# Graph layer on one core: the first group's user products in rounded and remainder parts, with buffers that share the left-over rows' place

## Chip, cores and metric

The kernel runs on 1 core of one Trainium2 chip. The metric is the device time of one execution in microseconds (us); before the change the median of 3 runs is 1091.55 us (1091.31 to 1091.62). The engines are TensorE (PE in the rows; PEld are its weight loads), VectorE (DVE), ScalarE (ACT), GpSimd (POOL) and SyncE (SP), which here only issues loads and stores.

## What is computed

```python
def ref(x, item_feat, adj, W_item, b_item, W_user, b_user):    # 10000 users, 10000 items, width 128
    u = maximum(layernorm(x, eps=1e-5), 0.0)
    h = item_feat @ W_item.T + b_item
    b = u @ W_user.T + b_user
    return x + relu(adj @ h + b)
```

Everything is float32. The adjacency is 10000 x 10000, 400 MB, read once.

## The kernel before

**Tiling.** The output is computed transposed, 128 features on the partitions and users along the free axis. Users are cut in five groups of 2048 (the last has 1808), each held in four PSUM banks of 512 (the very last bank has 272). Items are cut in 78 tiles of 128; 16 are left over. So the kernel walks 5 x 78 = 390 adjacency tiles of 128 items x 2048 users, 1 MB each. "Tile 60" below means tile 60 of its group.

**One tile.** SP loads it to one of eight slots of `a_ring` (L273), when tile n-8 has been used. ScalarE rounds it to `hi_ring` (float32r, four slots, L382), VectorE subtracts that from the tile and writes the remainder over the tile, as `lo_ring` (L496), and TensorE makes three matmuls for each of the four banks: h_lo x hi (L795), h_hi x hi (L796), h_hi x lo (L802). In the first 12 tiles of group 0 the pieces are halves or quarters (L390, L505).

**h.** In group 0 h is made beside the tiles, a trio of 128-item blocks at a time: three float32 matmuls (L721) at each third tile up to tile 69, which show as six instructions; then VectorE adds the bias (L523), ScalarE rounds (L403), VectorE takes the remainder (L534). The item features come in pieces of 384 KB (L265), one at each sixth tile in SP's order.

**The layer norm of x.** POOL issues loads of the users' rows to `rows` (L323; in group 0 four pieces of 256 KB when ScalarE has rounded 14, 16, 18 and 20 tiles: `ROWS_AT`), and of x to `y` (L326). VectorE sums rows (L572), TensorE makes the means (L740), VectorE centres (L580), ScalarE squares (L449), VectorE sums the squares (L587), TensorE makes variances (L746), VectorE adds eps, ScalarE takes the root, VectorE corrects and inverts it (L598 to L606), then scales and clamps (L612) and transposes (L619) one bank's users at a time to `normed_t`.

**The user product.** In group 0 it is one float32 matmul per bank (L754, `user_product`). In groups 1 to 4 it is made of parts (L762, L763, L765, `user_parts`): ScalarE rounds `normed_t` to `turned_hi` (L434), VectorE takes the remainder `turned_lo` (L566), and three float32r matmuls follow. These buffers lie over `items`, the item features' buffer, which is free only after group 0; W_user is rounded and subtracted early in group 1 (L417, L552).

**Left-over items.** Their 16 rows of the adjacency, three times, and two rows of ones for the bias come as four loads of 100 KB a group (L281, `load_rem`), ScalarE rounds them in two parts (L426), VectorE subtracts in two (L557), TensorE makes four matmuls of 50 rows (L776).

**Order.** Each engine runs its program in order. The place of each step is a tile number in the tables `FIRST` (group 0) and `LATER` (groups 1 to 4) and in constants such as `WU_AT`; a step stands before its tile's matmuls on TensorE and behind its tile's rounding or subtraction on ScalarE and VectorE. Steps for the four banks follow each other at `NORM_EVERY` = 5 tiles, the row sums at 2, the two parts of the left-over rows at 4.

## Time and profile before

| | us |
|---|---|
| median of 3 runs | 1091.55 (1091.31 to 1091.62) |
| the profiled execution | 1091.64 |
| its span, first to last instruction | 1089.8 |
| TensorE busy | 1084.4 |
| VectorE busy | 989.2 |
| ScalarE busy | 776.2 |
| POOL busy | 33.7 |
| chain that ended last | TensorE 99% |

Matmuls are pipelined and a matmul's end in the record is modelled: one shows as some 0.39 us while the next starts after about 0.23. So durations of TensorE are read here as distances between starts. A row of the timeline has the start and the time in us, the engine, line, operation, what it writes and reads, and, where the engine was idle before it, for how long and what ended that. The granted TensorE clock is full in all stretches.

### The profile page before, as it was taken

What the parts mean: (1) busy time and instruction counts of PE and PEld (TensorE: products, weight loads), DVE (VectorE), ACT (ScalarE), POOL (GpSimd) and SP (SyncE); (2) the same over time, 40 slices, a digit from 0 to 9 for tenths busy, and PEclk for the clock granted to TensorE, in tenths of its full rate; (3) what the DMA queues carried; (4) which work ended last, traced back from release to release, by engine and by line L of the source; (5) the groups of instructions that cost most, each with busy time, mean ns of one, the idle gap of its engine ahead of it and who ended that gap; (6) DMA issues with size and microseconds to landing.
All of it is one profiled execution on the core that took longest, in us unless ns stands there. A gap on an engine that the chain in (4) does not pass through costs nothing.

```text
span 1089.8 us, 12092 instructions
## 1 busy us (share of the span) xinstructions
PE 1084.4 (100%) x4952; PEld 900.4 (83%) x4952; DVE 989.2 (91%) x640; ACT 776.2 (71%) x492; POOL 33.7 (3%) x67
## 2 busy tenths in 40 slices
PE   9999999999999999999999999999999999999998
PEld 7888888788888888888888888888888888888887
DVE  7989999999899998898999988989999889899986
ACT  6767777667777776677777766777777667777764
POOL 0000000000000000000000000000000000000000
PEclk9999999999999999999999999999999999999999
DMA  9999999999999999999999999999999999999994
GB/s 387 416 425 407 424 426 375 372 358 410 410 399 407 379 400 388 376 415 400 400 395 390 399 380 357 424 413 394 403 387 399 363 364 413 385 414 393 384 346 149
DMA packets 65193, 422.98 MB, mean 388 GB/s; under 512 B 7977, under 2 KB 8778, under 8 KB 25202
## 3 DMA queue, kind: packets, MB, share of 16 engines
q1 hardware_dynamic: 60386, 407.61, 93.3%
q0 software_dynamic: 4608, 14.46, 4.3%
q8 instruction: 39, 0.64, 0.2%
q14 instruction: 16, 0.13, 0.0%
q10 hardware_dynamic: 144, 0.13, 0.0%
HBM read 417.04 MB, written 5.12 MB: 387 GB/s over the span
## 4 chain that ended last, share of the span: by engine, by line
PE 99%; DVE 0%; DMA 0%; ACT 0%; DVEq 0%; issue 0%
PE acc L795 32%; PE acc L802 32%; PE acc L796 32%; PE acc L721 2%; PE acc L762 0%; PE acc L765 0%; PE acc L763 0%; PE acc L754 0%; DMA wi_bi<-in_w_item_and_bias 0%; PE acc L776 0%; PE acc L706 0%; DVE y L630 0%; DVE lo_ring L505 0%; ACT hi_ring L390 0%; PE acc L740 0%; PE acc L746 0%
## 5 line engine op out<-in xcount | busy, mean ns | idle before, releaser
L382 ACT CAST hi_ring<-a_ring 128x2048 fp32r<-128x2048 f32 (+1 forms) x378 | 708.3, 1874 | 289.8 <-PE acc L802 266.2
L496 DVE TENSOR_TENSOR lo_ring<-a_ring,hi_ring 128x2048 fp32r<-128x2048 f32 (+1 forms) x378 | 840.7, 2234 | 78.8 <-ACT hi_ring L382 76.5
L795 PE MATMUL acc<-hi_ring,h_lo 128*128 128x512 f32 (+1 forms) x1560 | 604.5, 387 | 0.0
L802 PE MATMUL acc<-lo_ring,h_hi 128*128 128x512 f32 (+1 forms) x1560 | 599.9, 385 | 0.2 <-DVE lo_ring L505 0.2
L796 PE MATMUL acc<-hi_ring,h_hi 128*128 128x512 f32 (+1 forms) x1560 | 600.0, 385 | 0.0
L795 PEld LDWEIGHTS acc<-hi_ring,h_lo 128*128 128x128 f32 x1560 | 293.2, 188 | 59.7 <-issue 2.7
L802 PEld LDWEIGHTS acc<-lo_ring,h_hi 128*128 128x128 f32 x1560 | 292.9, 188 | 59.5 <-DVE lo_ring L505 0.8
L796 PEld LDWEIGHTS acc<-hi_ring,h_hi 128*128 128x128 f32 x1560 | 293.1, 188 | 57.8 <-issue 0.7
L505 DVE TENSOR_TENSOR lo_ring<-a_ring,hi_ring 128x1024 fp32r<-128x1024 f32 (+1 forms) x28 | 28.7, 1068 | 2.3 <-ACT hi_ring L390 2.3
L390 ACT CAST hi_ring<-a_ring 128x1024 fp32r<-128x1024 f32 (+1 forms) x28 | 24.5, 925 | 6.6 <-DMA a_ring<-in_adj_tiles 6.6
L326 POOL DMA_DIRECT2D y<-in_x_t x20 | 10.8, 542 | 530.0 <-ACT hi_ring L382 530.0
L721 PEld LDWEIGHTS acc<-wi_bi,items 128*128 128x128 f32 x156 | 21.9, 196 | 2.9 <-DMA wi_bi<-in_w_item_and_bias 0.9
L721 PE MATMUL acc<-wi_bi,items 128*128 128x128 f32 x156 | 22.4, 281 | 0.6 <-DMA wi_bi<-in_w_item_and_bias 0.6
L323 POOL DMA_DIRECT2D rows<-in_x_slices x20 | 10.9, 543 | 276.2 <-DVE normed_t L619 215.7
L523 DVE TENSOR_TENSOR h_full<-acc,wi_bi 128x384 f32<-128x384 f32 x25 | 13.8, 552 | 4.6 <-PE acc L721 4.4
L630 DVE SCALAR_TENSOR_TENSOR y<-acc,y 128x512 f32<-128x512 f32 (+1 forms) x20 | 12.7, 672 | 4.2 <-PE acc L802 4.2
L619 DVE STREAM_TRANSPOSE normed_t<-rows 128x512 f32<-128x512 f32 (+1 forms) x20 | 14.0, 700 | 0.7
L534 DVE TENSOR_TENSOR h_lo<-h_full,h_hi 128x384 fp32r<-128x384 f32 x25 | 13.8, 550 | 0.0
L403 ACT CAST h_hi<-h_full 128x384 fp32r<-128x384 f32 x25 | 12.7, 507 | 1.5 <-DVE h_full L523 1.5
L612 DVE SCALAR_TENSOR_TENSOR rows<-rows,stat 128x512 f32<-128x512 f32 (+1 forms) x20 | 13.5, 673 | 0.0
L580 DVE TENSOR_TENSOR rows<-rows,acc 128x512 f32<-128x512 f32 (+1 forms) x20 | 13.3, 667 | 0.0
L587 DVE TENSOR_REDUCE stat<-normed_t 128x16 f32<-128x512 f32 (+1 forms) x20 | 13.3, 666 | 0.0
(55 smaller groups left out, 153.9 us busy)
## 6 DMA issues: line engine op xcount, KB each, us to landing
a_ring<-in_adj_tiles SPq DMA_DIRECT2D x312, 1024.0 KB, 7.6
a_ring<-in_adj_tiles SPq DMA_DIRECT2D x78, 904.0 KB, 6.8
rows<-in_x_slices POOLq DMA_DIRECT2D x19, 256.0 KB, 6.9
y<-in_x_t POOLq DMA_DIRECT2D x19, 256.0 KB, 6.9
items<-in_item_t SPq DMA_DIRECT2D x12, 384.0 KB, 11.1
out_t<-y POOLq DMA_DIRECT2D x16, 256.0 KB, 7.8
a_rem<-in_adj_rem SPq DMA_DIRECT2D x20, 100.0 KB
out_t<-y SPq DMA_DIRECT2D x3, 256.0 KB, 2.4
```

The source lines that it names most:

```text
L382: nc.scalar.copy(hi_ring[:, n % S_SLOTS, cols], a_ring[:, n % A_SLOTS, cols]).then_inc(hi_written, 1)
L390: nc.scalar.copy(hi_ring[:, r, cols], a_ring[:, s, cols]).then_inc(part_hi if part < parts - 1 else hi_written, 1)
L496: nc.vector.tensor_tensor(lo_ring[:, s, cols], a_ring[:, s, cols], hi_ring[:, r, cols], ALU.subtract).then_inc(lo_written, 1)
L505: nc.vector.tensor_tensor(lo_ring[:, s, cols], a_ring[:, s, cols], hi_ring[:, r, cols], ALU.subtract).then_inc(part_lo if part < parts - 1 ...
L523: nc.vector.tensor_tensor(h_full[:, trio % H_BANKS, :, :], h_banks[trio % H_BANKS][:, 0:TRIO_W].rearrange("p (c d) -> p c d", d=HID), bi.u ...
L534: nc.vector.tensor_tensor(h_lo[:, trio * TRIO:(trio + 1) * TRIO, :], h_full[:, trio % H_BANKS, :, :], h_hi[:, trio * TRIO:(trio + 1) * TRI ...
L612: nc.vector.scalar_tensor_tensor(out=rows[:, b, :], in0=rows[:, b, :], scalar=0.0, in1=inv[:, b].unsqueeze(2).broadcast_to(wide(b)), op0=A ...
L619: nc.vector.transpose(normed_t[:, 0:n, :], rows[:, b, :]).then_inc(normed_t_ready, 1)
L721: last = nc.tensor.matmul(out, items[:, slot, at:at + P], wi, start=(m == 0 or (trio, m) == (0, 1)), stop=True, skip_group_check=True)
L795: nc.tensor.matmul(acc[k][:, 0:bank_w(g, k)], h_lo[:, c, :], hi, start=(c == 0), stop=False, skip_group_check=True)
L796: nc.tensor.matmul(acc[k][:, 0:bank_w(g, k)], h_hi[:, c, :], hi, start=False, stop=False, skip_group_check=True)
L802: last = nc.tensor.matmul(acc[k][:, 0:bank_w(g, k)], h_hi[:, c, :], lo, start=False, stop=(c == CHUNKS - 1), skip_group_check=True)
```

## The change

- The user products of group 0 are made by `user_parts` too; `user_product` is gone. ScalarE rounds `normed_t` at tiles 59, 64, 69, 74 of group 0, VectorE subtracts at 60, 65, 70, 75, and the products stand at 62, 67, 72, 77 (before: 61, 66, 71, 76).
- `turned_hi` and `turned_lo` lie over `a_rem` and `rem_parts`, the buffers of the left-over rows, and no more over `items`. So the left-over product stands ahead of the user products (tile 52 of group 0 and 46 of the others, before 66), ScalarE's first two roundings of a group wait for it, and the load of a group's left-over rows waits for the user products of the group before; it is issued at tile 24 instead of 30.
- W_user is rounded at tile 38 of group 0 instead of tile 4 of group 1.
- In group 0 all of the norm's steps stand two or three tiles earlier, and the rows' loads two. In the later groups norm, roundings and products stand two tiles later, and the left-over rows' rounding and subtraction 5 to 6 tiles earlier.

```diff
-REM_AFTER = 30
+REM_AFTER = 24
-WU_AT = 4
+WU_AT = 38
-ROWS_AT = 14
+ROWS_AT = 12
-FIRST = {"sum": 22, "mean": 30, "centre": 32, "square": 35, "sum_squares": 36, "wide_every": 4, "var": 51, "eps": 54, "sqrt": 57,
-         "root": 58, "norm": 59, "user": 61, "rem_round": 50, "rem_subtract": 52, "rem": 66}
+FIRST = {"sum": 20, "mean": 28, "centre": 30, "square": 33, "sum_squares": 34, "wide_every": 4, "var": 48, "eps": 51, "sqrt": 54,
+         "root": 55, "norm": 56, "turned": 59, "turned_lo": 60, "user": 62, "rem_round": 40, "rem_subtract": 43, "rem": 52}
 LATER = {"sum": 6, "mean": 15, "centre": 18, "square": 21, "sum_squares": 22, "wide_every": 5, "var": 40, "eps": 43, "sqrt": 46,
-         "root": 47, "norm": 50, "turned": 53, "turned_lo": 54, "user": 57, "rem_round": 38, "rem_subtract": 40, "rem": 66}
+         "root": 47, "norm": 52, "turned": 55, "turned_lo": 56, "user": 59, "rem_round": 32, "rem_subtract": 35, "rem": 46}
...
+        rem_at = nc.sbuf_base
         a_rem = sb("a_rem", [P, PAIR, BANK_W])
         rem_parts = sb("rem_parts", [P, PAIR, BANK_W], F32R)
+        turned_hi = nc.alloc_sbuf_tensor_at("turned_hi", [P, 2, BANK_W], F32R, offset=rem_at)
+        turned_lo = nc.alloc_sbuf_tensor_at("turned_lo", [P, BANK_W], F32R, offset=rem_at + 2 * BANK_W * 4)
...
-        items_at = nc.sbuf_base
         items = sb("items", [P, ITEM_SLOTS, PIECE_W])
-        turned_hi = nc.alloc_sbuf_tensor_at("turned_hi", [P, 2, BANK_W], F32R, offset=items_at)
-        turned_lo = nc.alloc_sbuf_tensor_at("turned_lo", [P, BANK_W], F32R, offset=items_at + 2 * BANK_W * 4)
...
             def load_rem(g):
                 if g > 0:
-                    sp.wait_ge(rem_lo_set, PAIR * g)
+                    sp.wait_ge(user_done, UNITS * g)
...
             def turned_round(g, k):
...
-                if v >= 2:
+                if k < 2:
+                    act.wait_ge(rem_used, g + 1)
+                else:
                     act.wait_ge(user_done, u - 1)
...
                     k = unit_at(c, at_of(g, "user"), NORM_EVERY)
-                    if k is not None and g == 0:
-                        user_product(g, k)
-                    elif k is not None:
+                    if k is not None:
                         user_parts(g, k)
```

Three places of the engines' order show what moved. On TensorE, around the first user product of group 0 (tile 61 before, tile 62 after), before:

```order
L802 MATMUL acc<-lo_ring,h_hi 128x512
L754 MATMUL acc<-normed_t,wu 128x512
L795 MATMUL acc<-hi_ring,h_lo 128x512
L796 MATMUL acc<-hi_ring,h_hi 128x512
L802 MATMUL acc<-lo_ring,h_hi 128x512
```

and after, where L783, L784 and L790 are the three matmuls of a bank:

```order
L790 MATMUL acc<-lo_ring,h_hi 128x512
L750 MATMUL acc<-turned_hi,wu_lo 128x512
L751 MATMUL acc<-turned_hi,wu_hi 128x512
L753 MATMUL acc<-turned_lo,wu_hi 128x512
L783 MATMUL acc<-hi_ring,h_lo 128x512
```

One float32 matmul has become three float32r matmuls. On SP, at tiles 18 to 36 of group 0 (L265 is a piece of the item features, L281 the left-over rows), the difference:

```order
 L265 DMA items<-in_item_t 128x768
 L273 DMA a_ring<-in_adj_tiles 128x2048 x6
-L265 DMA items<-in_item_t 128x768
-L273 DMA a_ring<-in_adj_tiles 128x2048 x6
 L281 DMA a_rem<-in_adj_rem 50x512 x4
 L265 DMA items<-in_item_t 128x768
```

The four loads stand six adjacency tiles and one piece of the item features earlier. On VectorE, from tile 58 to tile 61 of group 0 in the changed kernel (L496 are tiles, L534 and L523 belong to h, L611 and L615 are one bank's norm and transposition):

```order
L496 TENSOR_TENSOR lo_ring<-a_ring,hi_ring 128x2048
L523 TENSOR_TENSOR h_full<-acc,wi_bi 128x384
L496 TENSOR_TENSOR lo_ring<-a_ring,hi_ring 128x2048 x2
L534 TENSOR_TENSOR h_lo<-h_full,h_hi 128x384
L565 TENSOR_TENSOR turned_lo<-normed_t,turned_hi 128x512
L496 TENSOR_TENSOR lo_ring<-a_ring,hi_ring 128x2048
L523 TENSOR_TENSOR h_full<-acc,wi_bi 128x384
L611 SCALAR_TENSOR_TENSOR rows<-rows,stat 128x512
L615 STREAM_TRANSPOSE normed_t<-rows 128x512
```

and before, from tile 61 to tile 64, around the second bank's norm:

```order
L523 TENSOR_TENSOR h_full<-acc,wi_bi 128x384
L496 TENSOR_TENSOR lo_ring<-a_ring,hi_ring 128x2048 x2
L534 TENSOR_TENSOR h_lo<-h_full,h_hi 128x384
L496 TENSOR_TENSOR lo_ring<-a_ring,hi_ring 128x2048
L523 TENSOR_TENSOR h_full<-acc,wi_bi 128x384
L612 SCALAR_TENSOR_TENSOR rows<-rows,stat 128x512
L619 STREAM_TRANSPOSE normed_t<-rows 128x512
```

A subtraction of 512 columns has come in one tile ahead of each norm but the first, and one behind the last.

## Rows read from the trace of the kernel before

**Rows 1.** Head of the page: span, and busy time of TensorE and its weight loads.

```profile
span 1089.8 us, 12092 instructions
...
PE 1084.4 (100%) x4952; PEld 900.4 (83%) x4952; DVE 989.2 (91%) x640; ACT 776.2 (71%) x492; POOL 33.7 (3%) x67
```

**Rows 2.** Timeline, VectorE's subtraction and TensorE's first use, tiles 20, 24 to 26.

```profile
65.69 2.29 DVE L496 TENSOR_TENSOR lo_ring<-a_ring,hi_ring 128x2048 fp32r<-128x2048 f32 x1
...
69.05 0.39 PE L802 MATMUL acc<-lo_ring,h_hi 128*128 128x512 f32 x1
...
77.88 2.29 DVE L496 TENSOR_TENSOR lo_ring<-a_ring,hi_ring 128x2048 fp32r<-128x2048 f32 x1 [0.91 <-ACT hi_ring L382]
...
81.15 2.28 DVE L496 TENSOR_TENSOR lo_ring<-a_ring,hi_ring 128x2048 fp32r<-128x2048 f32 x1
...
81.33 0.40 PE L802 MATMUL acc<-lo_ring,h_hi 128*128 128x512 f32 x1
...
84.02 2.27 DVE L496 TENSOR_TENSOR lo_ring<-a_ring,hi_ring 128x2048 fp32r<-128x2048 f32 x1
...
84.09 0.39 PE L802 MATMUL acc<-lo_ring,h_hi 128*128 128x512 f32 x1
...
86.81 0.39 PE L802 MATMUL acc<-lo_ring,h_hi 128*128 128x512 f32 x1
```

**Rows 3.** Waits: who, for whom, us in total, times, longest us.

```profile
ACT hi_ring L382 <- DMA a_ring<-in_adj_tiles: 23.1, 25, 2.6
```

**Rows 4.** Timeline of TensorE, either side of a user product, tile 61, group 0.

```profile
190.96 0.40 PE L802 MATMUL acc<-lo_ring,h_hi 128*128 128x512 f32 x1
...
192.29 0.39 PE L796 MATMUL acc<-hi_ring,h_hi 128*128 128x512 f32 x1
```

**Rows 5.** Timeline of TensorE, group 1: around left-over product and user parts.

```profile
425.20 0.39 PE L802 MATMUL acc<-lo_ring,h_hi 128*128 128x512 f32 x1
...
426.52 0.39 PE L796 MATMUL acc<-hi_ring,h_hi 128*128 128x512 f32 x1
...
428.81 0.40 PE L802 MATMUL acc<-lo_ring,h_hi 128*128 128x512 f32 x1
...
429.75 0.39 PE L795 MATMUL acc<-hi_ring,h_lo 128*128 128x512 f32 x1
```

**Rows 6.** Timeline of TensorE, group 0: around a trio, around tile 66's pieces.

```profile
197.29 0.39 PE L802 MATMUL acc<-lo_ring,h_hi 128*128 128x512 f32 x1
...
198.41 0.40 PE L796 MATMUL acc<-hi_ring,h_hi 128*128 128x512 f32 x1
...
206.17 0.39 PE L802 MATMUL acc<-lo_ring,h_hi 128*128 128x512 f32 x1
...
209.01 0.39 PE L796 MATMUL acc<-hi_ring,h_hi 128*128 128x512 f32 x1
```

**Rows 7.** Timeline of ScalarE: roundings of tiles 20, 21 and 24, group 0.

```profile
63.74 1.92 ACT L382 CAST hi_ring<-a_ring 128x2048 fp32r<-128x2048 f32 x1 [0.84 <-DMA a_ring<-in_adj_tiles]
66.19 1.92 ACT L382 CAST hi_ring<-a_ring 128x2048 fp32r<-128x2048 f32 x1 [0.53 <-DMA a_ring<-in_adj_tiles]
...
75.93 1.92 ACT L382 CAST hi_ring<-a_ring 128x2048 fp32r<-128x2048 f32 x1 [1.62 <-DMA a_ring<-in_adj_tiles]
```

**Rows 8.** Groups by form: count, then busy us, mean ns, idle us before.

```profile
L566 DVE TENSOR_TENSOR turned_lo<-normed_t,turned_hi 128x512 fp32r<-128x512 f32 x15 | 10.3, 686 | 0.3
```

**Rows 9.** Timeline around tile 60: first norm, tile, piece of h; TensorE's use.

```profile
184.18 0.68 DVE L612 SCALAR_TENSOR_TENSOR rows<-rows,stat 128x512 f32<-128x512 f32 x1
...
185.53 2.25 DVE L496 TENSOR_TENSOR lo_ring<-a_ring,hi_ring 128x2048 fp32r<-128x2048 f32 x1
...
187.70 0.55 DVE L534 TENSOR_TENSOR h_lo<-h_full,h_hi 128x384 fp32r<-128x384 f32 x1
...
188.16 2.29 DVE L496 TENSOR_TENSOR lo_ring<-a_ring,hi_ring 128x2048 fp32r<-128x2048 f32 x1
...
188.88 0.40 PE L802 MATMUL acc<-lo_ring,h_hi 128*128 128x512 f32 x1
```

More of the change, by code:

```diff
@@ L428, in turned_round @@
             def turned_round(g, k):
-                u, v, n = g * UNITS + k, (g - 1) * UNITS + k, bank_w(g, k)
+                u, n = g * UNITS + k, bank_w(g, k)
                 act.wait_ge(normed_t_ready, u + 1)
-                if v >= 2:
+                if k < 2:
+                    act.wait_ge(rem_used, g + 1)
+                else:
                     act.wait_ge(user_done, u - 1)
-                nc.scalar.copy(turned_hi[:, v % 2, 0:n], columns_of(normed_t)[:, 0:n]).then_inc(turned_hi_set, 1)
+                nc.scalar.copy(turned_hi[:, k % 2, 0:n], columns_of(normed_t)[:, 0:n]).then_inc(turned_hi_set, 1)
             def square(g, k):
@@ L442, in square @@
                     act.wait_ge(squares_summed, u)
-                elif g == 1:
-                    act.wait_ge(user_done, u)
-                elif g > 1:
-                    act.wait_ge(turned_lo_set, u - UNITS)
+                elif g > 0:
+                    act.wait_ge(turned_lo_set, u)
                 nc.scalar.activation(squares[:, 0:n, :], rows[:, b, :], ACT.Square).then_inc(squares_ready, 1)
@@ L474, in _ @@
                         h_rem_round()
-                    if g == 1 and c == WU_AT:
+                    if g == 0 and c == WU_AT:
                         wu_round()
@@ L483, in _ @@
                         root_of_var(g)
-                    k = unit_at(c, at_of(g, "turned"), NORM_EVERY) if g > 0 else None
+                    k = unit_at(c, at_of(g, "turned"), NORM_EVERY)
                     if k is not None:
@@ L550, in wu_subtract_lo @@
                 dve.wait_ge(wu_hi_set, 1)
-                dve.wait_ge(user_done, UNITS)
                 nc.vector.tensor_tensor(wu_lo[:, :], wu[:, :], wu_hi[:, :], ALU.subtract).then_inc(wu_lo_set, 1)
@@ L560, in turned_subtract @@
             def turned_subtract(g, k):
-                u, v, n = g * UNITS + k, (g - 1) * UNITS + k, bank_w(g, k)
-                dve.wait_ge(turned_hi_set, v + 1)
-                if v > 0:
+                u, n = g * UNITS + k, bank_w(g, k)
+                dve.wait_ge(turned_hi_set, u + 1)
+                if k > 0:
                     dve.wait_ge(user_done, u)
-                nc.vector.tensor_tensor(turned_lo[:, 0:n], columns_of(normed_t)[:, 0:n], turned_hi[:, v % 2, 0:n],
+                nc.vector.tensor_tensor(turned_lo[:, 0:n], columns_of(normed_t)[:, 0:n], turned_hi[:, k % 2, 0:n],
                                         ALU.subtract).then_inc(turned_lo_set, 1)
@@ L615, in norm @@
                 dve.wait_ge(normed_ready, u + 1)
-                if g == 0 and k > 0:
-                    dve.wait_ge(user_done, u)
                 nc.vector.transpose(normed_t[:, 0:n, :], rows[:, b, :]).then_inc(normed_t_ready, 1)
@@ L673, in _ @@
                         empty(g - 1, 3)
-                    if g == 1 and c == WU_AT + 1:
+                    if g == 0 and c == WU_AT + 1:
                         wu_subtract_lo()
@@ L693, in _ @@
                         norm(g, k)
-                    k = unit_at(c, at_of(g, "turned_lo"), NORM_EVERY) if g > 0 else None
+                    k = unit_at(c, at_of(g, "turned_lo"), NORM_EVERY)
                     if k is not None:
@@ L747, in variance_product @@
                                  skip_group_check=True).then_inc(variance_done, 1)
-            def user_product(g, k):
-                if (g, k) == (0, 0):
-                    pe.wait_ge(user_loaded, 2 * 16)
-                pe.wait_ge(normed_t_ready, g * UNITS + k + 1)
-                columns = columns_of(normed_t)[:, 0:bank_w(g, k)]
-                nc.tensor.matmul(acc_of(g)[k][:, 0:bank_w(g, k)], wu[:, :], columns, start=False, stop=False,
-                                 skip_group_check=True).then_inc(user_done, 1)
             def user_parts(g, k):
-                u, v, n, out = g * UNITS + k, (g - 1) * UNITS + k, bank_w(g, k), acc_of(g)[k]
-                if v == 0:
+                u, n, out = g * UNITS + k, bank_w(g, k), acc_of(g)[k]
+                if u == 0:
                     pe.wait_ge(wu_lo_set, 1)
-                pe.wait_ge(turned_hi_set, v + 1)
-                nc.tensor.matmul(out[:, 0:n], wu_lo[:, :], turned_hi[:, v % 2, 0:n], start=False, stop=False, skip_group_check=True)
-                nc.tensor.matmul(out[:, 0:n], wu_hi[:, :], turned_hi[:, v % 2, 0:n], start=False, stop=False, skip_group_check=True)
-                pe.wait_ge(turned_lo_set, v + 1)
+                pe.wait_ge(turned_hi_set, u + 1)
+                nc.tensor.matmul(out[:, 0:n], wu_lo[:, :], turned_hi[:, k % 2, 0:n], start=False, stop=False, skip_group_check=True)
+                nc.tensor.matmul(out[:, 0:n], wu_hi[:, :], turned_hi[:, k % 2, 0:n], start=False, stop=False, skip_group_check=True)
+                pe.wait_ge(turned_lo_set, u + 1)
                 nc.tensor.matmul(out[:, 0:n], wu_hi[:, :], turned_lo[:, 0:n], start=False, stop=False,
```

## The prediction, as put on record before the changed kernel ran

> **What bounds the kernel now.** I read the head of the profile's page first: TensorE is busy for 1084.4 of the 1089.8 us of the span [rows 1]. The reader is to see that nothing but work taken off TensorE, or a stall put into it, can move the end. A busy PE need not be a PE at its pace, so I then read the timeline of PE for the distance between the starts of neighbouring matmuls. In the plain stretch that I use it is about 0.227 us (tile 20's L802 at 69.05, tile 25's at 84.09 and tile 26's at 86.81: between the last two lie 12 matmuls in 2.72 us) [rows 2]. The list of waits is read next, for ScalarE, which rounds each tile and stands between the loads and the rest: it waits for loads of the adjacency 25 times, 23.1 us in all [rows 3]. Nearly all of these waits belong to the first group, while the ring of eight tiles is being filled, and there the kernel is thin.
>
> So two things have to be worked out: what TensorE does less, and whether the moved loads and VectorE work run into the short lead that VectorE has over TensorE in the first group.
>
> **The TensorE sum.** A user product of group 0 is one float32 matmul in the code. Its cost is read between its neighbours: the L802 before it starts at 190.96, the L796 behind it at 192.29, 1.33 us apart, where two steps of 0.227 would be 0.45. The product costs 0.88 us [rows 4]. A product in parts, in group 1, runs from L802 at 428.81 to L795 at 429.75, 0.94, less one step: 0.71 us [rows 5]. The left-over product alone costs 1.32 - 0.45 = 0.87 (425.20 to 426.52) [rows 5]. The three matmuls of a trio cost 1.12 - 0.45 = 0.67 (197.29 to 198.41). At tile 66 a trio, a user product and the left-over product stand together and cost 2.84 - 0.45 = 2.39 (206.17 to 209.01), which is 0.03 less than 0.67 + 0.88 + 0.87 [rows 6]; the change separates them.
>
> Before: 3 x 0.88 + 2.39 = 5.03. After: 4 x 0.71 + 0.87 + 0.67 = 4.38. TensorE has 0.65 us less to do. Matmuls behind such a piece keep for one tile a pace about 0.003 us slower, so I hold 0.5 to 0.7 for possible. In the groups 1 to 4 the same matmuls are issued at other tiles: their left-over product goes from tile 66, next to nothing, to tile 46, next to nothing, the user parts from 57 to 59, and both cost what they did. Their sum is 0.
>
> The Trainium skill, page "TensorE: Matmul & The Clock Gate", section Back-to-back issue gap, gives N/2.4 + 2.5 ns for a warm matmul, 216 ns for 512 columns. By it three parts would cost 0.65 and the four products 0.9 us less instead of 0.7. The trace disagrees in every plain stretch, 0.227 for a step [rows 2], and the row decides.
>
> **What lies beside TensorE: ScalarE.** It gets four roundings of 512 columns more in group 0, of the kind of L434, and these lie where it waits for PE: it needs 1.92 us for a tile of 2.72 [rows 7]. Its new wait for the left-over product (tile 52, needed at 59) is met long before, as ScalarE is two to three tiles ahead of PE. Cost 0; behind it on ScalarE stand only the roundings of the ring, whose lead is several us there.
>
> **VectorE at the end of group 0.** It gets four subtractions, 0.69 us each for 15 of their kind in the later groups [rows 8]. The thin place before is tile 60, after the root and the first norm: its subtraction ends at 185.53 + 2.25 = 187.78, and PE wants it at 188.88, a lead of 1.10 [rows 9]. The root and norm move by three tiles, a whole trio period, so the same dip comes at tile 57. From there a round of five tiles costs VectorE, read from start to start, 5 x 2.17 (185.53 to 187.70), 5/3 x 2 x 0.46 for the pieces of h (187.70 to 188.16), 1.35 for a norm (184.18 to 185.53) [rows 9] and at most 0.69 for the new subtraction: 14.4 us. TensorE takes 5 x 2.72 + 5/3 x 0.67 + 0.71 = 15.4. The lead grows by 1.0 a round, so I take 0. If the cover is gone, the bound is 4 x 0.69 = 2.8 us; the lower end is 0, as nothing is taken from VectorE there. The left-over subtractions at 43 and 47 replace those at 52 and 56, where the lead is as large.
>
> **The loads and sums at tiles 12 to 27.** Here the change costs something. Tiles land 2.45 us apart while ScalarE waits for them (63.74 and 66.19, both ended by the load) [rows 7]: the DMA engines are full. A 256 KB piece of rows or x, a quarter of a tile, thus pushes later tiles back by 0.61 us, and the 400 KB of left-over rows push by 0.96. Four pieces of rows are issued two tiles earlier, and the x piece behind them with them. At tile 20 all five will have gone, before three had: the tile lands up to 2 x 0.61 = 1.2 us later. VectorE's lead there is 69.05 - (65.69 + 2.29) = 1.07 [rows 2]. The stall is then 0.15.
>
> The left-over rows go ahead of tile 24 instead of tile 30. VectorE's lead at tile 24 is 81.33 - (77.88 + 2.29) = 1.16; 0.96 of it goes and the earlier stall gives 0.15 back: 0.35. From tile 24 to 25 VectorE needs 81.15 - 77.88 = 3.27 (a subtraction of h and a row sum stand between them, in both kernels) and PE 84.09 - 81.33 = 2.76: 0.51 is lost, and the stall is about 0.15. To tile 26 VectorE needs 84.02 - 81.15 = 2.87 against 2.72, another 0.15. Before, the lead at tile 26 was 86.81 - (84.02 + 2.27) = 0.52, and nothing stalled [rows 2]. Together 0.45 us. The bound below is 0, if the transfers find gaps. The bound above is all of it on the path: 1.2 + 0.96 + one row sum moved ahead, at most 0.6 by the 3.27 + the 0.3 of the last two steps = 3.1. I take 0.45, by the leads, since they are read at the very tiles.
>
> That the pieces share the engines is also the rule of the Trainium skill, page "DMA: Bandwidth & Descriptors", section Issuing engines are not separate DMA queues: transfers of all issuing engines run on the same 16 and interleave. It speaks against this change, for by it the earlier rows on the POOL queue cannot pass beside the ring. The trace agrees as far as it can: ahead of tile 24, with a piece of items and two pieces from the POOL queue under way, ScalarE waits 1.62 us for the load, where it waits 0.53 for tile 21 [rows 7].
>
> **Queues and edges.** SP's new wait stands ahead of tile 24 of a group and asks for the user products of the group before, done about 18 tiles earlier; behind it wait the ring's loads, and they lose nothing. W_user's two halves move from group 1 to tile 38 and 39 of group 0, some 0.3 us each on engines with a lead. The first ten tiles and the tail after the last matmul are not touched.
>
> **The sum.** -0.65 + 0.45 = -0.2 us. The execution in the profile took 1091.64 (span 1089.8, so 1.84 outside), and this would give 1091.4; the median of 1091.55 gives 1091.35. I predict 1091.4. What a measurement of this kernel can tell from no change is about 0.2%, 2.2 us, so this is no change.
>
> **The rivals.**
> - *The leads hold* (chance 0.33). The saving of TensorE comes out whole: 1091.55 - 0.65 = 1090.9. For it: the lead of 1.07 and 1.16 nearly covers each delay, and pieces issued by POOL may be served slowly, not all at once. Against it: the lead of 0.52 at tile 26 is smaller than the 0.96 of the left-over rows.
> - *VectorE becomes the bound at the end of group 0* (0.09). If a round of five tiles has no 1.0 us to spare, up to 2.8 us of the new subtractions come on the path, less the lead of 1.1: 1091.55 - 0.65 + 1.7 = 1092.6, still within 0.2%.
> - *The ring runs dry* (0.04), the case on the slower side. At tiles 18 to 27 the leads cover nothing and the whole delay comes on the path: 1091.55 - 0.65 + 3.1 = 1094.0. It decides where the stalls of these tiles pass 2.8 us; with the lead of 1.16 spent first, tile 24 would have to land 4 us later than at 75.93. For it: the wait of 1.62 us shows what a few small loads do to one tile [rows 7]. Against it: the moved bytes add up to 2.2 us, and these leads are real in the rows.
> - *TensorE changes its pace* (0.02). With no float32 product in a group's last 17 tiles the products' neighbours would go faster than I read; for 0.2% that would have to be 2.2 us in 17 tiles, and no row shows such a pace.
>
> **How the numbers follow.** The forecast (stall and saving nearly cancel) has 0.52. Its own range is 1090.9 to 1092.1. With the first rival and the bound of the second the range is 1090.7 to 1092.6, and it leaves out about 0.1. Slower by over 0.2% is the third rival, 0.04; faster by over 0.2% is the last, 0.02; the rest, 0.94, is no change.
>
> **What would show it.** In the changed profile a user product of group 0 is three matmuls about 0.23 us apart, and the distance from the matmul before to the one behind is one step plus 0.71. Tile 20 and tiles 24 to 26 start late: the L802 of one of them begins as VectorE's subtraction ends, and ScalarE waits for its load at 24 longer than 1.62 us. From tile 57 to 77 PE has no wait. Groups 1 to 4 take the same time as before to 0.1 us. The forecast is wrong if the first group is longer than before by over 1 us, or shorter by over 1 us, or if any later group differs.

## The result, and the profile after

| | before | changed |
|---|---|---|
| median | 1091.62 us (12 runs, 1091.31 to 1092.46) | 1094.39 us (12 runs, 1093.36 to 1094.81) |
| ratio to before | | 1.0023, 95% interval 1.0016 to 1.0031 |
| profiled execution | 1091.64, span 1089.8 | 1094.03, span 1092.2 |

The changed kernel is slower by 0.23%, 2.8 us between the medians, and the interval leaves out 1. The forecast was 1091.4, the range 1090.7 to 1092.6, and "slower" had a chance of 0.04.

The head of the page after answers to [rows 1]. TensorE has four matmuls more, since the four user products of group 0 are now in parts, and is busy 1.5 us longer:

```profile
span 1092.2 us, 12109 instructions
...
PE 1085.9 (99%) x4956; PEld 901.1 (83%) x4956; DVE 990.1 (91%) x644; ACT 778.5 (71%) x496; POOL 33.7 (3%) x67
```

On so full an engine the busy time doesn't say where the loss is, because the end of a matmul that waits is also counted. The list of waits of the changed kernel (engine, line, for whom: us in total, times, longest) does. TensorE stands in it with new entries for VectorE's subtraction, and ScalarE's wait for tiles has become rarer than in [rows 3], 19 times and not 25, without the sum falling as much:

```profile
ACT hi_ring L382 <- DMA a_ring<-in_adj_tiles: 20.7, 19, 2.7
...
PEld acc L790 <- DVE lo_ring L496: 2.5, 4, 1.1
...
PE acc L790 <- DVE lo_ring L496: 0.9, 2, 0.6
```

To place it, I took the distance between the first matmuls of neighbouring tiles in both profiles. A stall is what such a distance has more than before:

| stretch | after minus before, us | forecast |
|---|---|---|
| up to tile 12 of group 0 | +0.43 | not touched |
| stalls at tiles 20, 24, 25, 26 | +0.38 +0.88 +0.57 +0.11 = +1.94 | +0.45 |
| the rest of group 0 | -0.53 | -0.65 |
| groups 1, 2, 3 | 0.00 each (216.49 and 216.49) | 0 |
| group 4 | +0.56 (190.27 to 190.83) | 0 |
| sum | +2.40 | -0.2 |

The first line can't be put down to the change: over the profiles of all kernels here the start of tile 12 lies anywhere from 44.8 to 45.7 us, in kernels with the rows of x at 14 (44.9 to 45.6) as in those with them at 12 (44.8 to 45.7).

**Group 0.** The timeline of ScalarE after (start, duration, what it waited for), tiles 20 to 24, answers to [rows 7]:

```profile
65.40 1.91 ACT L382 CAST hi_ring<-a_ring 128x2048 fp32r<-128x2048 f32 x1 [1.51 <-DMA a_ring<-in_adj_tiles]
67.82 1.91 ACT L382 CAST hi_ring<-a_ring 128x2048 fp32r<-128x2048 f32 x1 [0.51 <-DMA a_ring<-in_adj_tiles]
70.26 1.92 ACT L382 CAST hi_ring<-a_ring 128x2048 fp32r<-128x2048 f32 x1
74.01 1.92 ACT L382 CAST hi_ring<-a_ring 128x2048 fp32r<-128x2048 f32 x1 [1.83 <-DMA a_ring<-in_adj_tiles]
78.63 1.91 ACT L382 CAST hi_ring<-a_ring 128x2048 fp32r<-128x2048 f32 x1 [2.70 <-DMA a_ring<-in_adj_tiles]
```

The left-over rows are issued ahead of tile 24. Here tile 23 lands 3.75 us behind tile 22, and tile 24 another 4.62 us later, where a plain tile takes 2.44. VectorE and TensorE then, tiles 24 to 26, against [rows 2]:

```profile
80.57 2.29 DVE L496 TENSOR_TENSOR lo_ring<-a_ring,hi_ring 128x2048 fp32r<-128x2048 f32 x1 [2.21 <-ACT hi_ring L382]
83.85 2.28 DVE L496 TENSOR_TENSOR lo_ring<-a_ring,hi_ring 128x2048 fp32r<-128x2048 f32 x1
86.71 2.27 DVE L496 TENSOR_TENSOR lo_ring<-a_ring,hi_ring 128x2048 fp32r<-128x2048 f32 x1
```

```profile
82.92 0.50 PE L790 MATMUL acc<-lo_ring,h_hi 128*128 128x512 f32 x1 [0.63 <-DVE lo_ring L496]
86.18 0.50 PE L790 MATMUL acc<-lo_ring,h_hi 128*128 128x512 f32 x1 [0.26 <-DVE lo_ring L496]
...
89.06 0.48 PE L790 MATMUL acc<-lo_ring,h_hi 128*128 128x512 f32 x1
```

Each first use begins 0.05 to 0.08 us behind the end of the subtraction (80.57 + 2.29 = 82.86, and 82.92): the lead of 1.16 us is gone. VectorE's own steps are those of before, 3.28 and 2.86 us (3.27 and 2.87 in [rows 2]). Only the landing of tile 24 moved.

**Group 4.** Its banks are 272 columns wide at the end. The first of the three matmuls on such a bank, once per tile, before:

```profile
1014.52 0.28 PE L795 MATMUL acc<-hi_ring,h_lo 128*128 128x272 f32 x1
...
1016.95 0.28 PE L795 MATMUL acc<-hi_ring,h_lo 128*128 128x272 f32 x1
```

and after, first behind the left-over product at tile 46, then behind the user products at tiles 59 and 64:

```profile
1012.46 0.29 PE L783 MATMUL acc<-hi_ring,h_lo 128*128 128x272 f32 x1
...
1014.93 0.29 PE L783 MATMUL acc<-hi_ring,h_lo 128*128 128x272 f32 x1
...
1055.54 0.28 PE L783 MATMUL acc<-hi_ring,h_lo 128*128 128x272 f32 x1
...
1057.96 0.28 PE L783 MATMUL acc<-hi_ring,h_lo 128*128 128x272 f32 x1
```

A tile takes 2.47 us at first and 2.42 later, with no wait in the rows. The step is 2.467 us from tile 47 up to tile 58 and 2.420 before the left-over product: 11 x 0.047 = 0.52 of the 0.56.

### The profile page after: what moved, and what is told of

Read it like the earlier page. It is cut to its first block, busy times and chain, and to the rows that moved or that the text cites. A ratio compares the mean times of both kernels' runs of the same rounds, so it can differ in the third digit from the quotient of the medians.

```text
span 1092.2 us, 12109 instructions
## 1 busy us (share of the span) xinstructions
PE 1085.9 (99%) x4956; PEld 901.1 (83%) x4956; DVE 990.1 (91%) x644; ACT 778.5 (71%) x496; POOL 33.7 (3%) x67
## 4 chain that ended last, share of the span: by engine, by line
PE 96%; DMA 2%; DVE 1%; ACT 0%; DVEq 0%; issue 0%
PE acc L783 31%; PE acc L790 31%; PE acc L784 31%; DMA a_ring<-in_adj_tiles 2%; PE acc L717 1%; PE acc L750 0%; PE acc L753 0%; PE acc L751 0%; DVE lo_ring L496 0%; DMA wi_bi<-in_w_item_and_bias 0%; PE acc L764 0%; ACT hi_ring L382 0%; PE acc L702 0%; DVE y L626 0%; DVE lo_ring L505 0%; PE acc L736 0%
## 5 line engine op out<-in xcount | busy, mean ns | idle before, releaser
L496 DVE TENSOR_TENSOR lo_ring<-a_ring,hi_ring 128x2048 fp32r<-128x2048 f32 (+1 forms) x378 | 840.6, 2233 | 80.3 <-ACT hi_ring L382 78.4
L783 PE MATMUL acc<-hi_ring,h_lo 128*128 128x512 f32 (+1 forms) x1560 | 604.0, 387 | 0.0
L790 PE MATMUL acc<-lo_ring,h_hi 128*128 128x512 f32 (+1 forms) x1560 | 600.8, 385 | 1.1 <-DVE lo_ring L496 0.9
L784 PE MATMUL acc<-hi_ring,h_hi 128*128 128x512 f32 (+1 forms) x1560 | 600.2, 385 | 0.0
L790 PEld LDWEIGHTS acc<-lo_ring,h_hi 128*128 128x128 f32 x1560 | 293.0, 188 | 62.0 <-DVE lo_ring L496 2.5
L783 PEld LDWEIGHTS acc<-hi_ring,h_lo 128*128 128x128 f32 x1560 | 293.2, 188 | 58.8 <-issue 1.8
L784 PEld LDWEIGHTS acc<-hi_ring,h_hi 128*128 128x128 f32 x1560 | 293.3, 188 | 57.8
L523 DVE TENSOR_TENSOR h_full<-acc,wi_bi 128x384 f32<-128x384 f32 x25 | 13.8, 551 | 5.0 <-PE acc L717 4.9
L615 DVE STREAM_TRANSPOSE normed_t<-rows 128x512 f32<-128x512 f32 (+1 forms) x20 | 14.0, 701 | 0.7
L534 DVE TENSOR_TENSOR h_lo<-h_full,h_hi 128x384 fp32r<-128x384 f32 x25 | 13.7, 549 | 0.0
L611 DVE SCALAR_TENSOR_TENSOR rows<-rows,stat 128x512 f32<-128x512 f32 (+1 forms) x20 | 13.4, 672 | 0.0
L565 DVE TENSOR_TENSOR turned_lo<-normed_t,turned_hi 128x512 fp32r<-128x512 f32 (+1 forms) x20 | 13.4, 671 | 0.0
```

The source lines that it names most:

```text
L496: nc.vector.tensor_tensor(lo_ring[:, s, cols], a_ring[:, s, cols], hi_ring[:, r, cols], ALU.subtract).then_inc(lo_written, 1)
L523: nc.vector.tensor_tensor(h_full[:, trio % H_BANKS, :, :], h_banks[trio % H_BANKS][:, 0:TRIO_W].rearrange("p (c d) -> p c d", d=HID), bi.u ...
L534: nc.vector.tensor_tensor(h_lo[:, trio * TRIO:(trio + 1) * TRIO, :], h_full[:, trio % H_BANKS, :, :], h_hi[:, trio * TRIO:(trio + 1) * TRI ...
L565: nc.vector.tensor_tensor(turned_lo[:, 0:n], columns_of(normed_t)[:, 0:n], turned_hi[:, k % 2, 0:n], ALU.subtract).then_inc(turned_lo_set, 1)
L615: nc.vector.transpose(normed_t[:, 0:n, :], rows[:, b, :]).then_inc(normed_t_ready, 1)
L783: nc.tensor.matmul(acc[k][:, 0:bank_w(g, k)], h_lo[:, c, :], hi, start=(c == 0), stop=False, skip_group_check=True)
```

## The experiments

My theory after this reading was: nearly all of the loss is the left-over rows loaded ahead of tile 24, and the rows of x at tile 12 add little. A rival held the rows of x responsible, as they delay tile 20. A third cause, for the last 0.5 us, was the left-over product at tile 46 in the last group.

### The left-over rows back to tile 30

```diff
-REM_AFTER = 24
+REM_AFTER = 30
```

> The changed kernel with the left-over rows' loads back at tile 30 in all groups (REM_AFTER 30); rows, sums and all else as changed. Theory 1 (the left-over rows ahead of tile 24 push it back by some 2.4 us, not 0.96): TensorE's stalls at tiles 24 to 26 of group 0, 1.56 us in the changed kernel's profile, go; 1094.4 - 1.5 = 1092.9. The stall of about 0.4 at tile 20 stays. Rival (the row sums two tiles earlier cost the lead, whoever loads): stalls at tiles 24 to 26 stay at 1 us or more, 1094.

Measured: 1092.45 us (1092.18 to 1093.05, 11 runs), ratio 1.0006 (0.9997 to 1.0015). The stalls of tiles 18 to 26 are 0.72 us, nearly all of them at tile 20; those at 24 to 26 are gone. ScalarE's rows, tiles 22 to 24:

```profile
70.50 1.91 ACT L382 CAST hi_ring<-a_ring 128x2048 fp32r<-128x2048 f32 x1
72.93 1.91 ACT L382 CAST hi_ring<-a_ring 128x2048 fp32r<-128x2048 f32 x1 [0.52 <-DMA a_ring<-in_adj_tiles]
76.28 1.92 ACT L382 CAST hi_ring<-a_ring 128x2048 fp32r<-128x2048 f32 x1 [1.44 <-DMA a_ring<-in_adj_tiles]
```

From tile 22 to 24 it is 5.78 us where the changed kernel has 8.37: the 400 KB cost 2.6 us of landing, and not the 0.96 by their bytes. The kernel is 1.9 us faster than the changed one, which is 0.5 more than expected.

### The rows of x back to tile 14

```diff
-ROWS_AT = 12
+ROWS_AT = 14
```

> The changed kernel with the first group's rows loaded from 14 rounded tiles on (ROWS_AT 14) instead of 12; the left-over rows stay at tile 24. Theory 1: the stall at tile 20 (0.4 us) goes, but as the five pieces now land up to tile 23, tile 24 is as late as in the changed kernel and the stall there takes back what was won: stalls at 24 to 26 of 1.6 to 2.0, total 1094.0 to 1094.4. Rival (the rows' loads are the main cost): under 1093.

Measured: 1094.17 us (1093.58 to 1094.51), ratio 1.0021 (1.0012 to 1.0030). The stall at tile 20 is gone, but the one at tile 24 grows to 1.63, 2.31 us at tiles 24 to 26: the delays meet at one tile. The rival, which had asked for under 1093, falls.

### Both back

```diff
-REM_AFTER = 24
+REM_AFTER = 30
-ROWS_AT = 12
+ROWS_AT = 14
```

> The changed kernel with both loads where they were before (REM_AFTER 30, ROWS_AT 14), row sums and all compute steps as changed. Theory 1: no stall of TensorE between tiles 12 and 57 of group 0 above 0.1 us, group 0 is 0.5 us shorter than before from tile 12 on, and what is left over the kernel before is the slower pace of group 4 (0.55): about 1091.6 to 1091.9. Rival (sums moved ahead are part of the stall): 0.3 to 0.6 us of stall stay at tiles 24 to 26, 1092.3.

Measured: 1091.66 us (1091.36 to 1093.23), ratio 1.0002 (0.9993 to 1.0011). No stall in tiles 18 to 26, one of 0.30 at tile 31, where left-over rows, x and a centring stand together. The whole 2.8 us come back. In this profile the stall of 0.30 and the 0.56 of group 4 outweigh TensorE's saving of 0.5 by 0.4, and tile 12 starts 0.36 earlier than before. The rows of x are not as harmless as I had thought: between this kernel and the one with the left-over rows alone at 30 they make 0.8 us (1091.66 and 1092.45), while with the left-over rows at 24 they make only 0.2 (1094.17 and 1094.39).

### One number in the kernel before

```diff
-REM_AFTER = 30
+REM_AFTER = 24
```

> The kernel before with one number changed: the left-over rows' loads at tile 24 instead of 30 (REM_AFTER 24). Theory 1: tile 24 lands 2.1 to 2.4 us later, its lead of 1.16 is spent and TensorE stalls for 1.0 to 1.6 us at tiles 24 to 26: 1091.6 + 1.3 = 1092.9. As the record had it (0.96 us of delay by their bytes): a stall of 0.3 at most, 1091.9.

Measured: 1094.41 us (1093.29 to 1095.44), ratio 1.0022 (1.0014 to 1.0031); the kernel before, measured beside it, 1091.69 (33 runs). Nothing else of the change is in this kernel, and it is as slow as the changed one. I had the direction right and the size too small: 1.0 to 1.6 us of stalls and 1092.9 were expected. The stalls are 0.69, 1.78, 0.54 and 0.13 us at tiles 23 to 26; the later groups are those of before. Its list of waits:

```profile
DVE lo_ring L496 <- ACT hi_ring L382: 78.6, 173, 3.6
...
ACT hi_ring L382 <- DMA a_ring<-in_adj_tiles: 25.6, 26, 4.0
...
PEld acc L802 <- DVE lo_ring L496: 2.9, 3, 2.0
```

The longest wait of ScalarE for a tile is 4.0 us; in [rows 3] it is 2.6. So the cause is shown for the main part, by taking it out of one kernel (1.9 of the 2.8 us) and putting it alone into the other (2.7 us). "Nearly all" was too much: the stall at tile 20 and the pace of group 4 are the rest, less what TensorE saves.

### The left-over product at tile 46 in the kernel before

```diff
-... "rem": 66}
+... "rem": 46}
```

(in LATER)

> The kernel before with one number changed: the left-over product of groups 1 to 4 at tile 46 instead of 66. Theory 1 (behind the left-over product, matmuls of 50 rows, the last group's tiles keep a slower pace until another product stands among them: 2.467 us instead of 2.420 for the 11 tiles from 47 to 57 in the changed kernel): group 4 gets 0.5 us longer (here from tile 47 to 56), groups 0 to 3 stay, 1092.2 in all. Rival (the slower pace came from VectorE's or ScalarE's steps at other tiles): group 4 stays at 190.27, 1091.7.

Measured: 1092.23 us (1091.99 to 1092.85), ratio 1.0006 (0.9998 to 1.0015). The times alone can't tell this from no change; the rows can. Groups 1 to 3 are unchanged, group 4 takes 190.74, +0.47. The bank rows of group 4:

```profile
1013.20 0.29 PE L795 MATMUL acc<-hi_ring,h_lo 128*128 128x272 f32 x1
...
1015.67 0.29 PE L795 MATMUL acc<-hi_ring,h_lo 128*128 128x272 f32 x1
...
1018.14 0.29 PE L795 MATMUL acc<-hi_ring,h_lo 128*128 128x272 f32 x1
```

The slower pace, 2.47 us a tile, comes with the left-over product alone. This profile also has stalls of 0.38 and 0.10 at tiles 25 and 26 of group 0, which nothing in the edit explains. Tile 24 is rounded at 76.38 us here and at 75.40 to 76.04 in the four other kernels with the same loads ahead of it, and the lead at tile 25 before is only 0.66.

### Why 400 KB cost 2.6 us

Four loads bring 50 partitions x 2 KB each. Three explanations stood against each other: the short packets (1a) or the number of loads; an uneven share, as 50 rows do not divide over the 16 DMA engines and 64 would (1b); or that a load which reaches only half of the partitions is slow, whatever its packets (1c, formed after the third of these runs). All five kernels are the changed one with other loads of the left-over rows; where 64 or 128 rows are moved, the rows are padded and 512 KB are loaded.

```diff
 two loads of 50 x 4 KB
+sp.dma_start(a_rem[row:row + REM_ROWS, :, :], adj_rem[g, part]).then_inc(rem_loaded, 16)
 one load of 128 x 4 KB
+sp.dma_start(a_rem[:, :, :], adj_rem[g]).then_inc(rem_loaded, 16)
 four loads of 64 x 2 KB
+sp.dma_start(a_rem[row:row + ROWS_BLOCK, k // PAIR, 0:n], adj_rem[g * ACC_BANKS + k, :, 0:n]).then_inc(rem_loaded, 16)
 two loads of 128 x 2 KB
+sp.dma_start(a_rem[:, half, :], adj_rem[g, :, half, :]).then_inc(rem_loaded, 16)
 two loads of 64 x 4 KB
+sp.dma_start(a_rem[half, :, :], adj_rem[g, half, :, :]).then_inc(rem_loaded, 16)
```

> The changed kernel with the same bytes of left-over rows (400 KB a group) laid out so that each partition's are 4 KB in one run: two loads of 50 partitions instead of four with 2 KB each. Theory 1a (the loads cost by their small packets, 0.118 us for one of 2 KB against 0.31 for one of 8 KB): tile 24 lands about 1.7 us after its undisturbed time instead of 2.4, stalls at 24 to 26 fall from 1.6 to about 0.9, 1093.7. Theory 1b (they cost since 50 partitions load the 16 DMA engines unevenly): the delay stays at 2.2 to 2.4 us and the time at 1094.4.

> The changed kernel with the left-over rows of a group in one load of all 128 partitions, 4 KB each, 28 of the partitions being filling: 512 KB instead of 400. Theory 1a (packets): delay of tile 24 about 1.25 x that of the 4 KB layout, near 2.1 us, 1094. Theory 1b (uneven engines): the delay falls to about that of its bytes, 1.2 us, and the stalls at 24 to 26 to 0.4 us, 1093.2.

> The changed kernel with four loads of left-over rows as before, but of 64 partitions each instead of 50 (14 of them filling, 512 KB in all, 2 KB a partition). Theory 1b (50 partitions load the DMA engines unevenly, 128 or 64 evenly): the loads delay tiles 23 and 24 by about 1.25 us as the single load of 128 did, stalls at 24 to 26 under 0.4 us, 1092.2. Rival (it was one load against four that won): the delay stays at 2.5 us or more, since there are more bytes, and the time at 1094.4 or above.

> The changed kernel with the left-over rows in two loads of 128 partitions x 2 KB (512 KB a group, 28 partitions filling). Theory 1c (a load that reaches only 50 or 64 of the partitions moves at a third of the rate, whatever its rows' length): delay of tiles 23 and 24 about 1.25 us, as with one load of 128, stalls at 24 to 26 under 0.2 us, 1092.1. Rival (2 KB packets or more than one load cost): delay of 2.5 us or more, 1094 or above.

> The changed kernel with the same 512 KB in two loads of 64 partitions x 4 KB, the lower half and then the upper. Theory 1c: delay of tiles 23 and 24 by 3 to 4 us, as with four loads of 64, stalls of 2.5 us or more, 1094 to 1095. Rival (packets or count of loads): as h1_two128 or better, 1092.1.

Measured. "Landing" is the time from tile 22 to 24 on ScalarE beyond the 5.78 us without these loads, "stalls" are all those of tiles 18 to 26, of which the ones at 18 to 22 (0 to 1.2 us) do not come from these loads:

| left-over rows loaded as | KB | landing, us | stalls, us | median, us (range) | ratio to before |
|---|---|---|---|---|---|
| 4 of 50 x 2 KB (changed) | 400 | 2.6 | 1.94 | 1094.39 | 1.0023 |
| 2 of 50 x 4 KB | 400 | 3.2 | 3.40 | 1095.05 (1094.11 to 1095.59) | 1.0029 (1.0019 to 1.0040) |
| 4 of 64 x 2 KB | 512 | 3.9 | 3.96, 1.1 of it by the clock | 1093.99 (1093.71 to 1095.65) | 1.0022 (1.0013 to 1.0031) |
| 2 of 64 x 4 KB | 512 | 3.7 | 3.13 | 1094.62 (1094.31 to 1095.39) | 1.0027 (1.0017 to 1.0038) |
| 2 of 128 x 2 KB | 512 | 1.3 | 0.46 | 1092.09 (1091.88 to 1092.35) | 1.0002 (0.9994 to 1.0011) |
| 1 of 128 x 4 KB | 512 | 1.2 | 0.04 | 1092.08 (1091.86 to 1092.56) | 1.0003 (0.9994 to 1.0012) |

Three expectations missed here: the two loads of 4 KB packets came out slower than either theory said (1095.05), and four loads of 64 didn't give the 1092.2 of the uneven share; the single load of 128 did better than its 1093.2.

The four loads of 64 need a remark of their own. Their profiled execution is the slowest of eleven, 1095.65 where the median is 1093.99, and in it TensorE's clock fell: from 84.0 to 87.4 us the granted clock is 0.50, the lower of its two levels (1.2 GHz). Just before, TensorE had waited 0.19 and 1.53 us for the rounding and the subtraction of tile 24. TensorE's row with the longer wait, and the window behind it:

```profile
83.72 0.60 PE L790 MATMUL acc<-lo_ring,h_hi 128*128 128x512 f32 x1 [1.53 <-DVE lo_ring L496]
84.00:86.00 2.00, 2.00 (x6) 1.50 (x6) 2.00 (x3) 1.69 (x1) 0.54 (x1) 0.50 1.04 438
```

Its matmuls stand 0.43 us apart there and not 0.23. At tile 26 the subtraction is then done 1.11 us ahead of its use, where the lead is 0.05 with two loads of 64: so about 1.1 of the 3.96 us is the clock's, and not the loads'. In no other profile here does the granted clock fall between the first tile and the last, so no other row of the table has this in it.

More bytes over all partitions cost half of what fewer bytes cost over less than half of them. 512 KB are 0.5 of a tile, 0.5 x 2.45 = 1.2 us: loads that reach 128 partitions cost about their bytes, with packets of 2 or 4 KB, one load or two. Loads of 64 partitions cost three times as much in both packet lengths, and with 64 rows as with 50. The packets and the uneven share fall, the latter against what I had expected, and what is left is the half of the partitions. Each landing is of one profile, and the same stretch without left-over rows varies from 6.25 to 7.02 us over five kernels with the rows of x at tile 14, so a landing is good to some 0.8 us; the 2.4 us between 64 and 128 partitions, and the 2 us between their medians, are clear of that. The last pair is the cleanest: ScalarE's rows of tiles 22 to 24, first two loads of 128 x 2 KB, then two of 64 x 4 KB, the same bytes:

```profile
69.69 1.92 ACT L381 CAST hi_ring<-a_ring 128x2048 fp32r<-128x2048 f32 x1
72.14 1.91 ACT L381 CAST hi_ring<-a_ring 128x2048 fp32r<-128x2048 f32 x1 [0.53 <-DMA a_ring<-in_adj_tiles]
76.78 1.91 ACT L381 CAST hi_ring<-a_ring 128x2048 fp32r<-128x2048 f32 x1 [2.73 <-DMA a_ring<-in_adj_tiles]
```

```profile
69.68 1.92 ACT L382 CAST hi_ring<-a_ring 128x2048 fp32r<-128x2048 f32 x1
74.07 1.91 ACT L382 CAST hi_ring<-a_ring 128x2048 fp32r<-128x2048 f32 x1 [2.48 <-DMA a_ring<-in_adj_tiles]
79.16 1.91 ACT L382 CAST hi_ring<-a_ring 128x2048 fp32r<-128x2048 f32 x1 [3.18 <-DMA a_ring<-in_adj_tiles]
```

The windows show the same as a rate (the stretch, its length, busy us of PE, PEld, DVE, ACT and POOL with their counts, the granted clock, the DMA share, GB/s). Two loads of 128, two loads of 64, and the changed kernel, each while the loads are under way:

```profile
71.00:73.00 2.00, 2.00 (x13) 1.77 (x12) 2.00 (x3) 1.47 (x2) 0.00 (x0) 1.00 1.08 435
```

```profile
71.00:73.00 2.00, 2.00 (x14) 1.75 (x13) 2.00 (x3) 0.59 (x1) 0.00 (x0) 1.00 1.07 210
```

```profile
71.00:73.00 2.00, 2.00 (x13) 1.77 (x12) 2.00 (x3) 1.18 (x1) 0.00 (x0) 1.00 1.08 271
```

The DMA engines show as fully busy in all three; only the GB/s tell them apart. Over the whole stretch of the landing, 128 partitions and then 64:

```profile
70.00:77.00 7.00, 7.00 (x36) 5.84 (x35) 7.00 (x6) 3.75 (x3) 0.00 (x0) 1.00 1.03 423
```

```profile
70.00:77.00 7.00, 7.00 (x35) 5.85 (x34) 6.57 (x6) 3.51 (x2) 0.00 (x0) 1.00 1.04 294
```

These rates account for most of the factor of three. The load has its own bytes, 1.2 us; and as long as its packets are under way, everything else is slow too. Over these 7 us, 129 of 423 GB/s are missing, 7 x 129/423 = 2.1 us. Together that is 3.3 of the 3.7 us; for the changed kernel (338 GB/s in the same window) it is 0.96 + 1.4 = 2.4 of its 2.6. The packets in the traces say the same: the 8 KB packets of the ring's own tiles take 309 ns each beside loads of 128 partitions, and 416 ns on average beside the two loads of 64. The 4 KB packets of these two take 275 ns on average, and 159 in the single load of 128.

### What the findings give

Here the changed kernel has the rows of x at tile 14, the left-over load of group 0 at tile 36, behind the filling of the ring, and the left-over product of the later groups at tile 39, early enough for another product (the variance's, at tile 40) to follow at once. The second kernel adds the single load of 128 partitions (at tile 34).

```diff
+REM_AFTER_FIRST = 36
-ROWS_AT = 12
+ROWS_AT = 14
 LATER:
-"rem_round": 32, "rem_subtract": 35, "rem": 46}
+"rem_round": 28, "rem_subtract": 31, "rem": 39}
-                    if c == REM_AFTER:
+                    if c == (REM_AFTER if g > 0 else REM_AFTER_FIRST):
```

> The changed kernel with three places moved: rows' loads from 14 rounded tiles on; the first group's left-over rows loaded at tile 36 (the other groups' stay at 24); the left-over product of groups 1 to 4 at tile 39, just ahead of the variance product (tile 40), its rounding at 28 and subtraction at 31. Theory 1: no stall of TensorE from tile 12 on, the saving of 0.55 us of the products in parts comes out whole, and group 4 keeps the pace of 2.420 after the variance product, 190.27 to 190.3: 1091.65 - 0.55 = 1091.1, and a profile whose group 0 takes 0.5 us less from tile 12 on. Rival (a stall moves to another tile as each load is moved): one stall of 0.3 us or more in group 0, 1091.5.

> f2_best with the left-over rows of a group in one load of 128 partitions, the first group's at tile 34. Theory 1: nothing left to win by it but the safety of the leads; group 0 from tile 12 on takes 198.2 us as in f2_best, group 4 190.27, 1090.8 with less spread. Rival: the 28 partitions of filling (112 KB a group) cost where the DMA engines are full, 1091.2.

Measured: 1090.83 us (1090.73 to 1091.94), ratio 0.9994 (0.9985 to 1.0003), the kernel before measured beside it 1091.54; and 1091.29 (1090.74 to 1091.82), ratio 0.9995 (0.9986 to 1.0004). In the profile of the first there are no stalls at tiles 18 to 31, group 0 from tile 12 to its end is 198.17 us against 198.66, and group 4 is 190.27 as before:

```profile
span 1089.2 us, 12109 instructions
...
PE 1083.9 (100%) x4956; PEld 900.5 (83%) x4956; DVE 990.0 (91%) x644; ACT 778.6 (71%) x496; POOL 33.8 (3%) x67
```

TensorE is busy 0.5 us less than in [rows 1]. The saving is thus real in the profile, but at 0.05% no comparison of times here can tell it from nothing. Padding to one wide load adds nothing once the load stands where there is lead: in its profile group 0 takes 198.14 from tile 12 and group 4 190.27. Its median is the 1091.29 of which the rival had spoken (1091.2), but no row shows a cost of the padding.

## Why the prediction was wrong

**Right: TensorE's saving.** A user product of group 0 in parts costs 0.71 us; the matmul before begins at 196.95 and the one behind at 197.89, 0.94 less one step of 0.23. The rest of group 0 is shorter by 0.53, and by 0.5 in the kernels without stalls: less than the 0.65 of the sum, at the lower edge of the 0.5 to 0.7 held possible.

```profile
196.95 0.40 PE L790 MATMUL acc<-lo_ring,h_hi 128*128 128x512 f32 x1
197.18 0.40 PE L750 MATMUL acc<-turned_hi,wu_lo 128*128 128x512 f32 x1
197.42 0.40 PE L751 MATMUL acc<-turned_hi,wu_hi 128*128 128x512 f32 x1
197.66 0.40 PE L753 MATMUL acc<-turned_lo,wu_hi 128*128 128x512 f32 x1
197.89 0.39 PE L783 MATMUL acc<-hi_ring,h_lo 128*128 128x512 f32 x1
```

**Right: VectorE at the end of group 0, and ScalarE.** The dip came at tile 57, as said, and as deep: the subtraction ends at 182.14 and its first use is at 183.27, a lead of 1.13 us where 1.10 had been read at tile 60 before. From there a round of five tiles gives 1.41, 2.85, 2.31 and 4.56 us at tiles 62, 67, 72 and 77, which is not a steady 1.0 a round but nearly that on average. PE has no wait from tile 57 to 77. The rival "VectorE becomes the bound" fell.

```profile
179.89 2.25 DVE L496 TENSOR_TENSOR lo_ring<-a_ring,hi_ring 128x2048 fp32r<-128x2048 f32 x1
...
183.27 0.40 PE L790 MATMUL acc<-lo_ring,h_hi 128*128 128x512 f32 x1
```

**Nearly right: tile 20.** The two pieces of rows were to make it land 1.2 us later. It is 1.4: ScalarE begins at 65.40 and not at 63.74, less the 0.27 by which it is late already at tile 12. Over all profiles here it is 1.6 on average (63.3 to 63.7 with the rows of x at tile 14, 64.8 to 65.6 with them at 12). The lead of 1.07 was read rightly, and the stall is 0.38 where 0.15 was said. The mechanism holds, the size is off by 0.2 here; other kernels with these rows at 12 stall there by 0 to 0.7.

**Wrong: the price of the left-over rows.** This is the step that failed: "the 400 KB of left-over rows push by 0.96", that is 400 KB in proportion to a tile that takes 2.45 us. They push by 2.6. The leads and VectorE's steps around it were right: put 2.6 into the same working and tile 20 stalls by 0.15 as before, tile 24 by 2.6 - 0.15 - 1.16 = 1.29 (0.88 measured), tile 25 by 0.51 (0.57), tile 26 by 0.15 (0.11). That gives 2.1 us of stalls, where 1.94 were measured and 0.45 were forecast. One figure, too small by a factor of 2.7, makes the whole difference.

The row that would have told was in the trace of before, where the same loads stand ahead of tile 30. ScalarE's tiles 28 to 30:

```profile
86.02 1.92 ACT L382 CAST hi_ring<-a_ring 128x2048 fp32r<-128x2048 f32 x1 [0.59 <-DMA a_ring<-in_adj_tiles]
89.80 1.91 ACT L382 CAST hi_ring<-a_ring 128x2048 fp32r<-128x2048 f32 x1 [1.87 <-DMA a_ring<-in_adj_tiles]
94.24 1.91 ACT L382 CAST hi_ring<-a_ring 128x2048 fp32r<-128x2048 f32 x1 [2.52 <-DMA a_ring<-in_adj_tiles]
```

The steps are 3.78 and 4.44 us where a plain one is 2.45: 3.3 us late over two tiles. A piece of the item features, 384 KB, stands there too and is 0.92 by its bytes; 2.4 us are left for the left-over rows. The later runs bear that out: these two steps take 5.77 to 5.95 us in all ten kernels that have no left-over rows there, and 7.73 to 8.60 in the four that have. The rate in that stretch was low too, beside a stretch just before it:

```profile
87.00:91.00 4.00, 4.00 (x22) 3.39 (x21) 4.00 (x3) 2.13 (x2) 0.00 (x0) 1.00 1.05 295
78.00:84.00 6.00, 6.00 (x31) 5.05 (x30) 6.00 (x6) 5.09 (x5) 0.54 (x1) 1.00 1.01 427
```

I priced a moved load by its bytes, though its own cost could be read where it stood. Before, it cost TensorE nothing since the leads at 29 to 31 had grown; the zero effect there was not a zero price.

The bound above had the same fault. 3.1 us was built from 1.2 + 0.96, with the same price by bytes, and the rival "the ring runs dry" was refused because "the moved bytes add up to 2.2 us". It named the right place and side, and its 1094.0 is the nearest of all to the 1094.4 measured. Its chance of 0.04 rested on that one figure. But its own condition, stalls over 2.8 us, was not met: the leads did cover a part, the stalls are 1.94, and group 4 gives another 0.56. That its number came so near is luck.

**Wrong: the later groups.** "Their sum is 0" holds for groups 1 to 3 to 0.01 us, and not for group 4, +0.56. The text had seen that matmuls behind a left-over product keep a slower pace, and said "for one tile". That holds in groups whose banks are all 512 columns wide, where tile 46 takes 2.86 us and tile 47 again 2.72. In the last group it lasts until the next user product, at tile 59. The forecast's own tests ("wrong if any later group differs", or if the first is longer by over 1 us) caught both. With both figures put right the sum is -0.65 + 2.1 + 0.55 = +2.0, 1093.5 us, and the profiles have 1.97 from tile 12 on. Of the 0.9 us left to the median, 0.4 is that tile 12 starts earlier in the profile before, and 0.4 that the profiled execution of the changed kernel is faster than its median; what moves single executions by that much I can't say.

**The rule that was passed over.** The prediction used a rule of sharing by bytes. The Trainium skill, page "DMA: Bandwidth & Descriptors", section Rules for kernel authors, has one that bore on this case: the most bandwidth comes with 128 partitions, and of two transfers to disjoint partition halves it says "Don't bother", use one transfer of 128. The runs agree with the advice, and give the price: 3.7 us as two halves against 1.3 us as loads of 128 for the same 512 KB.

**Open.** Why packets to half of the partitions are slow, and slow down those beside them, no view here shows. Nor is it settled why the price of the same 400 KB varies, 2.6 us in the changed kernel, and with the rows of x at tile 14 rather 2.9 and 3.5: from tile 22 to 24 the kernel before takes 6.46 us, the changed one with these rows at 14 takes 9.34, and the kernel before with its one number changed 9.94. A part is the spread of single profiles, 6.25 to 7.02 us for this stretch without the loads. For the pace of group 4, which property of the left-over product sets it, and what of another product ends it, was not tried.

## What to carry to other kernels

Price a transfer by what the tiles around it lose where it now stands, not by its bytes: look at the landing steps and the GB/s of that stretch, since the DMA share reads as full for a slow transfer too. If a small load reaches few partitions, either spread it over all 128, padding included, or put it where the consumers' lead is well above its measured price. When one run of a set is odd, look at the granted clock before you read its stalls. When a step moves from one stage to another, check it in every stage that has another shape; here the narrow last group had its own answer.
